# Decoder block: attention products with 64-column stationary values in the two self-attention stages with heads of 32

## The reference, cut to what matters

```python
q, k, v = split(x @ Wq), split(x @ Wk), split(x @ Wv)      # [8, 16, 112, 32]
scores = einsum('bhqd,bhkd->bhqk', q, k) * scale           # layer 0: times a causal 0/1 mask
attn = softmax(scores, axis=-1)
out = einsum('bhqk,bhkd->bhqd', attn, v)                   # [8, 16, 112, 32]
return out.transpose(0, 2, 1, 3).reshape(8, 112, 512) @ Wo
```

## Time and profile before

| | |
|---|---|
| median of 3 runs | 2807.86 us (2807.6 to 2813.41) |
| span of the profiled execution | 2808.8 us |
| PE busy | 2598.3 us, 93% |
| PE weight loads | 2142.5 us, 76% |
| DVE busy | 1717.6 us, 61% |
| ACT busy | 1129.9 us, 40% |
| POOL busy | 764.2 us, 27% |
| mean granted TensorE clock | 0.953 |

### The profile page before, as it was taken

One profiled execution on the slowest core, in us unless ns is written; L12 is line 12 of the kernel. 1 busy time (PEld: TensorE's weight loads), 2 busy tenths in 40 slices (PEclk: granted clock), 3 DMA queues, 4 the chain that ended last, 5 costly groups with the idle time before them and its releaser, 6 DMA issues. The chain is left out here.

```text
span 2808.8 us, 49906 instructions
## 1 busy us (share of the span) xinstructions
PE 2598.3 (93%) x15563; PEld 2142.5 (76%) x15564; DVE 1717.6 (61%) x3341; ACT 1129.9 (40%) x2434; POOL 764.2 (27%) x791
## 2 busy tenths in 40 slices
PE   8999799979899999799996998989999999899998
PEld 7888677768688777578875876767777788788887
DVE  4537767669777666576665576864444435656564
ACT  2103255523343324455543233755444421444343
POOL 3213100024333235423233101740000012345455
PEclk9999999999899979899997998999999989999999
DMA  5454122125622045477773432353212031666664
GB/s 191 152 144 99 36 87 73 45 73 162 175 73 63 17 145 188 141 216 219 197 225 86 127 71 75 117 174 91 87 49 87 8 129 58 164 158 150 159 150 82
DMA packets 289285, 332.98 MB, mean 119 GB/s; under 512 B 147446, under 2 KB 202694, under 8 KB 287313
## 3 DMA queue, kind: packets, MB, share of 16 engines
q1 hardware_dynamic: 217904, 252.57, 28.8%
q0 software_dynamic: 20640, 51.74, 9.3%
q10 hardware_dynamic: 50560, 26.34, 3.2%
HBM read 233.86 MB, written 96.72 MB: 118 GB/s over the span
## 5 line engine op out<-in xcount | busy, mean ns | idle before, releaser
L898 PE MATMUL e_psum<-e_up_hi,hT_hi 128*128 x672 | 246.8, 367 | 21.3 <-DVE hT_lo L867 12.7
L900 PE MATMUL e_psum<-e_up_hi,hT_lo 128*128 x672 | 238.1, 354 | 0.0
L899 PE MATMUL e_psum<-e_up_lo,hT_hi 128*128 x672 | 238.0, 354 | 0.0
L898 PEld LDWEIGHTS e_psum<-e_up_hi,hT_hi 128*128 128x128 f32 x672 | 128.7, 192 | 43.8 <-issue 32.4
L1565 POOL TENSOR_TENSOR self_a_p<-self_a_p,self_a_mx 112x448 f32<-112x448 f32 x96 | 96.0, 1000 | 205.2 <-DVE self_a_mx L1622 205.2
L794 ACT ACTIVATE e_gate<-e_psum 128x352 f32<-128x352 f32 (+1 forms) x86 | 44.4, 516 | 260.1 <-PE e_psum L900 256.0
L873 DVE TENSOR_TENSOR hT_lo<-e_psum,hT_hi 128x256 fp32r<-128x256 f32 (+2 forms) x138 | 55.7, 435 | 143.4 <-ACT hT_hi L812 135.6
L1656 ACT ACTIVATE self_a_p<-self_a_p 112x448 f32<-112x448 f32 x128 | 71.6, 575 | 165.0 <-POOL self_a_p L1565 113.9
L900 PEld LDWEIGHTS e_psum<-e_up_hi,hT_lo 128*128 128x128 f32 x672 | 128.6, 191 | 11.7
L899 PEld LDWEIGHTS e_psum<-e_up_lo,hT_hi 128*128 128x128 f32 x672 | 128.8, 192 | 9.9
L1786 PEld LDWEIGHTS joint_psum<-x_v,joint_a_pt 125*112 125x112 f32 (+1 forms) x1024 | 120.1, 179 | 19.8 <-issue 14.4
(11 more groups left out here) (563 smaller groups left out, 7385.1 us busy)
## 6 DMA issues: line engine op xcount, KB each, us to landing
e_up_raw<-in_L_ffn_w SPq DMA_DIRECT2D x64, 512.0 KB, 4.9
e_up_raw<-in_L_ffn_w SPq DMA_DIRECT2D x64, 352.0 KB
e_dn_raw<-in_L_ffn_w SPq DMA_DIRECT2D x16, 1024.0 KB, 15.0
q_all<-p_p_t_stage ACTq DMA_DIRECT2D x56, 256.0 KB
e_dn_raw<-in_L_ffn_w SPq DMA_DIRECT2D x16, 512.0 KB
x_q<-q_all SPq DMA_DIRECT2D x8, 896.0 KB
v_ctx<-front_c_v_stage SPq DMA_DIRECT2D x24, 250.0 KB
x_others<-k_ctx SPq DMA_DIRECT2D x8, 750.0 KB, 4.7
```

The costliest lines, as they stand in the source:

```text
L898: pe.matmul(out, lhs[0], rhs[0], start=k == 0, stop=False)
L899: pe.matmul(out, lhs[0], rhs[1], start=False, stop=False)
L900: return pe.matmul(out, lhs[1], rhs[0], start=False, stop=k == n_k - 1)
```

## The change

For heads of 32 (`turned`) the operands of the value product change places. The stationary operand is now a slice of 64 columns of the value tile (the 33 of the head and 31 of the next), the probabilities stream by in 112 columns. The result has value columns on partitions and tokens along the free axis. Heads j = 0, 2 write to partitions 0 to 63, heads j = 1, 3 to partitions 64 to 127, so a step's 8 heads fill one bank [128 x 448]. ACT copies this bank to SBUF once per step (tile `ot`), PE turns it back with 4 transposes into the other bank, and DVE takes the reciprocal of 8 sums and multiplies 256 columns once per step. All of this comes one step later than before (LE = 3), the output ring has 3 places and not 4, and the value tile's padding is 32 columns and not 128.

```diff
-        RING, LT, LE = 6, 2, 2
+        turned = dh == 32
+        RING, LT, LE = 6, 2, 3 if turned else 2
...
-        O_RING, per_group = 4, 512 // (group * dh)
+        O_RING, per_group = 3 if turned else 4, 512 // (group * dh)
...
+                if turned:
+                    for i, n in pair(step, LE)[0:1]:
+                        pe.wait_ge(ot_ready, i // W + 1)
+                        reuse(pe, o_evac, i // W)
+                        for x in range(2 * W):
+                            last = pe.transpose(ps[0:T, o_banks[1], x * 128:(x + 1) * 128], ot[:, x * T:(x + 1) * T], core.ident[:, :])
+                        last.then_inc(back_done, 1)
                 yield
                 for i, n in pair(step, LT):
...
                     pe.wait_ge(pt_ready, i + 1)
+                    if turned:
+                        u = i % W
+                        reuse(pe, ot_ready, i // W)
+                        for j in range(group):
+                            first, at = kv_of(n, j) * (dh + 1), (2 * u + j // 2) * T
+                            last = pe.matmul(ps[64 * (j % 2):64 * (j % 2) + 64, o_banks[0], at:at + T], v[:, b % 2, first:first + 64],
+                                             pt[:, u, j, :], start=True, stop=True)
+                        last.then_inc(pv_done, 1)
+                        continue
...
+                for i, n in pair(step, LE)[0:1] if turned else []:
+                    unit, made = i // per_group, i // W
+                    back = ps[0:T, o_banks[1], :].rearrange("p (u j e) -> p u j e", u=W, j=group)
+                    dve.wait_ge(back_done, made + 1)
+                    dve.reciprocal(rinv[:, :, :], back[:, :, :, dh]).then_inc(rinv_ready, 1)
+                    dve.wait_ge(rinv_ready, made + 1)
...
+                    dve.tensor_tensor(to, back[:, :, :, 0:dh].rearrange("p u j d -> p j u d"),
+                                      rinv[:, :, :].rearrange("p u j -> p j u").unsqueeze(3).to_broadcast([T, group, W, dh]),
+                                      ALU.mult).then_inc(o_evac, 1)
...
+                for i, n in pair(step, LT)[0:1] if turned else []:
+                    act.wait_ge(pv_done, i + W)
+                    reuse(act, back_done, i // W)
+                    act.copy(ot[:, :], ps[:, o_banks[0], 0:W * 2 * T]).then_inc(ot_ready, 1)
```

More of the change, by code:

```diff
@@ L1485, in __init__ @@
             k = g.sb(f"{name}_k", [128, 2, ck, T])
-            v = g.sb(f"{name}_v", [T, 2, n_kv * (dh + 1) + 128])
+            v = g.sb(f"{name}_v", [T, 2, n_kv * (dh + 1) + (32 if turned else 128)])
         def landed(b):
@@ L1495, in __init__ @@
         rinv = g.sb(f"{name}_rinv", [T, 2, group])
-        O_RING, per_group = 4, 512 // (group * dh)
+        O_RING, per_group = 3 if turned else 4, 512 // (group * dh)
         self.o = o = g.sb(f"{name}_o", [T, O_RING, 512])
-        self.evacs_per_group, self.o_ring = per_group, O_RING
+        self.evacs_per_group, self.o_ring = per_group // W if turned else per_group, O_RING
+        if turned:
+            ot = g.sb(f"{name}_ot", [128, W * 2 * T])
+            ot_ready, back_done = g.sem(f"{name}_ot_ready"), g.sem(f"{name}_back_done")
         qk_in, v_in = g.sems(f"{name}_qk_in", 2), g.sems(f"{name}_v_in", 2)
@@ L1627, in vector @@
                 yield
-                for i, n in pair(step, LE):
+                for i, n in pair(step, LE)[0:1] if turned else []:
[4 more added lines that the diff above has]
+                    dve.wait_ge(rinv_ready, made + 1)
+                    if n == 0:
+                        reuse(dve, self.o_used, unit - O_RING + 1)
+                    to = o[:, unit % O_RING, :].rearrange("p (j r d) -> p j r d", r=4, d=dh)[:, :, n:n + W, :]
+                    dve.tensor_tensor(to, back[:, :, :, 0:dh].rearrange("p u j d -> p j u d"),
+                                      rinv[:, :, :].rearrange("p u j -> p j u").unsqueeze(3).to_broadcast([T, group, W, dh]),
+                                      ALU.mult).then_inc(o_evac, 1)
+                for i, n in pair(step, LE) if not turned else []:
                     unit, part = i // per_group, i % per_group
@@ L1635, in vector @@
                         reuse(dve, self.o_used, unit - O_RING + 1)
[L1636 to L1639, removed]
+                    to = o[:, unit % O_RING, part * group * dh:(part + 1) * group * dh].rearrange("p (h d) -> p h d", h=group)
                     dve.tensor_tensor(to, out[:, :, 0:dh], rinv[:, i % 2, :].unsqueeze(2).to_broadcast([T, group, dh]),
```

## The result

The changed kernel takes 2813.93 us (median of 20 runs, 2809.81 to 2818.98), the kernel before 2809.8 us in 20 runs of the same kind. The ratio is 1.0018, with an interval of 1.0011 to 1.0024: slower by some 5 us, where 2800 us and a gain of 8 were forecast. Two of the segments grew. From the first matmul of `self0` to the first of the next segment it is 193.6 us against 190.7; for `self3` 215.3 against 212.0. The rest differs by up to 3 us, save the last segment, which was 6.5 us shorter in this execution. These are single executions. Over the ten kernels profiled here, segments that no change touched scatter as much: the last one takes 413.8 to 420.5 us, the self-attention at about 740 us, whose heads are not of 32, 239.3 to 244.6. So a difference of 3 us in one segment shows little by itself; what carries weight is how all the kernels fall into groups, as told under the experiments.

What follows compares the result with a forecast made beforehand. PE was taken to bound about a third of each segment's 16 steps, PE and DVE in turn the rest. Per step -0.69 + 0.44 = -0.25 us, times 32, took 8.0 from 2808.8: 2800 us, range 2792 to 2812.

Steps and rivals of the forecast that it cites:

- The value product: A step's 16 matmuls on PE: 0.97 us plus 0.09 at entry, 1.06 where it cost 1.75, -0.69 us per step.
- Rival one: Column tiles of the value product follow one another: PE +0.41 us per step, 2818 us; chance 0.13.
- Rival two: Value product's weight loads in the open: 2872 us at most, 2840 with loads of half that length; chance 0.02.
- The four transposes back: On PE behind the scores, in full-array form, 128 streamed columns each: +0.44 us per step.
- DVE: One reciprocal and one product per step, 0.55 us in place of 0.83: -0.28 us; no gain counted from shorter waits.
- ACT: One more copy per step, some 0.45 us; just fits with 0.3 us to spare for handovers, cost nothing.
- rival three: ACT sets the pace: value product waits 0.3 to 0.5 us in half the steps, 2806 us; chance 0.16 with small other losses.
- Lag and rings: A step's output comes one step later: cost nothing; 1.4 us per segment if the cover failed.
- rival five: Granted clock shifts as PE has less work in DVE stretches: 2806 or 2794 us; chance 0.08, half on either side.
- The other segments: Segments other than the two changed: unchanged to a few tenths, else the explanation by these steps is wrong.
- The sum: Two segments of 16 steps, 32 x 0.25 = 8.0 us gained: 2800.8 us against the profiled execution, 2800 as median.

## Why the prediction was wrong, point by point

- *The value product*, forecast 0.97 us and 0.09 at its entry, 1.06 together: right to 0.01 us. It is 0.92, with 0.09 in the group ahead of it and 0.05 in the transposes behind it. One comparison on the way was wrong: the 0.97 us of the scores are not under half of the 1.54 us of 16 full-array matmuls but 63% of them. Nothing hung on it. Rival one (tiles in sequence, 0.13) did not come. Rival two, the rule of the Trainium skill's page "TensorE: Matmul & The Clock Gate", section "Part 3: Packing small matmuls — row/col tiling", that a weight load overlaps matmuls in flight only in another row group, would have made the product over 2 us; the trace disagrees: 0.92 us for 16 matmuls whose loads, all of the same 112 rows, take 0.136 us each on average, 2.2 us together. (The lower figure of that rival, 2840 us, is a slip; its own terms give 2847.)
- *The four transposes back*, forecast +0.44 us of work: 0.46 us of work (262.04 to 262.50 us, a step of the trace after), but this is the step that failed. It was priced as four instructions, with no wait. They also bring a wait of their own, for DVE's product of the step before, since all of them use one bank: 9.3 us in `self0`, 4.0 us net of the waits that it replaced. The prediction never said what stands behind it. The list of the order shows both: the waiting row with `self0_a_o_evac`, and the first output matmul right under it. That such a wait could bind could be had from the rows at hand: PE's scores wait for L1618, which ties PE to DVE's place in its order, and what DVE has to do from there until its product is done (1.6 us in the trace after) could have been set against PE's 0.97 us of scores. The runs show the step as the cause from both sides: with the transposes half a step later the kernel is 15 us faster, and the wait alone makes the kernel before 7 us slower.
- *DVE*, forecast 0.55 us for the pair: 280.43 to 281.00, 0.57 us. "It now waits for the transposes in the first half and no longer for the value product" was right too: the wait for L1602 has no successor among DVE's waits. It was counted as room for a gain. The same shift seen from PE was the loss.
- *ACT*, "just fits": right. PE has no listed wait in `self0` for its copies before a value product. In `self3` it has one of 2.1 us, just over the 2 us that were to be the sign of rival three, but the kernel before has 1.8 us of it. With the transposes moved, ACT's order changed nothing.
- *Lag and rings*, cost nothing: not right in the details. The turning of the attention output asked for `o_evac` before as well, but had no listed wait for DVE's product between 200 and 350 us; it waits 3.3 us in the changed kernel and 6.8 with the transposes moved. One step more of lag did use up the slack of the output part.
- *The clock*, rival five: its sign came, 0.88 from 270 to 290 and from 290 to 310 us where 0.98 and 1.00 had been, and the prediction gave it 0.04 on this side. It came with the wait, not by itself: the wait alone brings it too, with the old product and no less work on PE. In `self0` PE's standing and the lower clock have about equal parts in the 7.1 us between the changed kernel and the one with the transposes moved: PE stands 3.3 us less, and is busy 3.9 us less with the same instructions (171.02 and 167.16 us, at 0.93 and 0.96). So even a prediction that had priced the wait would have had only part of the loss.
- *The other segments* were to be unchanged to a few tenths, or the explanation by these steps would be wrong. They differ by up to 6.5 us. The sign was too strict: over the kernels profiled here those segments scatter by as much, whatever the edit.
- *The sum*: 8 us of gain were forecast, 5 lost. With the one step mended the kernel takes 2799.18 us, against the 2800 forecast. That agreement is partly luck: the gain is 10 us beside a kernel before of 2809.47, not 8 beside 2807.86, the segments account for only 6.6 of it, and a part of it is a better clock, which the forecast did not count.

## What to carry to other kernels

Price a moved or added step by what it waits for and by what is queued behind it on its engine, not by its instructions alone: here four transposes of 0.46 us turned a gain of 10 us into a loss of 5 by asking for a buffer half a step too soon, in every second step in front of 12 ready matmuls. Do not read the price off the new wait's own row either: it replaced other waits (9.3 us, 4.0 net), and it cost about as much again in granted clock. Compare standing time, busy time and clock of the whole stretch. Where an engine is let go at one point of another engine's order and waits for a later point of the same order, count the work between the two points on both engines; if the waiting engine has less, it stands in every step where the other sets the pace. A shared buffer that is written half a step earlier needs its reader half a step earlier too, or a second buffer, or a place behind work that fills the time. Only the last was tried here.

## What the runs showed of the hardware

Float32 products with 64 stationary columns and 112 streamed ones, alternately into both halves of the columns, run at 0.92 us for 16 matmuls, as fast as row tiles (0.97), where 8 in a row in one half make it 1.35 us; with pairs of heads in one half it is 0.96. Going into the tiled form costs the group ahead 0.09 us (0.48 against 0.39 for four transposes), coming out of it the eight transposes behind 0.05 (0.91 against 0.86). And where PE stood 0.5 to 0.7 us, in most steps once and in every second step twice, the granted clock was 0.88 over 40 us, from 270 to 310; in the kernel before it was 0.98 from 270 to 290 us (of that trace) and 1.00 from 290. With the wait alone in the kernel before it was 0.91 and 0.85 over these two stretches. Which of these short stands brings it down is not settled: with the transposes moved PE stood 0.83 us ahead of 273.59 us and 0.76 ahead of 277.21, and the clock from 270 to 290 us was 1.00.
